# A decoder on one core: smaller four-bit scales, one product on GpSimd, and another start for the slots

## The reference

```python
def fp4_quant_dequant(x):                      # the part that the change touches
    xb = x.reshape(shape[:-1] + (shape[-1] // 16, 16))
    scale = jnp.max(jnp.abs(xb), axis=-1, keepdims=True) / 6.0
    scale = jnp.maximum(scale, jnp.float32(1e-12))
    xn = xb / scale
    idx = jnp.searchsorted(_MID, jnp.abs(xn))  # 0.25 0.75 1.25 1.75 2.5 3.5 5.0
    return (_GRID[idx] * jnp.sign(xn) * scale).reshape(shape)   # 0 0.5 1 1.5 2 3 4 6

gate = fp4_linear(x, w_gate)                   # both sides quantized
y = fp4_linear(x, w_up)
h = jax.nn.silu(gate) * y
return fp4_linear(h, w_down)

x = _layernorm(x + L0_attn(x)); x = _layernorm(x + L0_xattn(x, ctx)); x = _layernorm(x + L0_ffn(x))
x = _layernorm(x + L1_attn(x)); x = _layernorm(x + L1_xattn(x, ctx)); x = _layernorm(x + L1_ffn(x))
```

## Time and profile before

| what | us |
|---|---|
| median of 3 runs (lowest, highest) | 1032.47 (1031.52, 1033.19) |
| the profiled execution | 1034.37 |
| its span, from first to last instruction | 1032.5 |
| PE busy / PEld busy | 902.5 / 719.3 |
| DVE busy | 637.8 |
| ACT busy | 487.1 |
| POOL busy | 273.2 |

### The profile page before, as it was taken

How to read it: one execution, slowest core, us unless ns; L and a number is a source line. 1 busy time by engine, 2 the same in 40 slices (tenths; PEclk the granted TensorE clock), 3 DMA queues, 4 the chain that set the end, 5 groups by cost and what they waited for, 6 DMA issues and landing times.

```text
span 1032.5 us, 20172 instructions
## 1 busy us (share of the span) xinstructions
PE 902.5 (87%) x7498; PEld 719.3 (70%) x7498; DVE 637.8 (62%) x1909; ACT 487.1 (47%) x1127; POOL 273.2 (26%) x416
## 2 busy tenths in 40 slices
PE   4569889998999989999999989999999999598980
PEld 3346667776776766677688767777888888587870
DVE  4998877666575778786776668787653533015006
ACT  2335445445645554454454556555555454143430
POOL 4322311211152133221213222242221224024222
PEclk9678999999999988999999999999999999799995
DMA  9998000000010000000000030232112268797954
GB/s 330 386 330 296 1 2 6 11 11 11 17 46 22 17 17 21 17 6 11 7 11 22 16 113 22 83 129 98 58 46 83 79 202 274 308 331 276 377 194 161
DMA packets 39426, 114.88 MB, mean 111 GB/s; under 512 B 5464, under 2 KB 21600, under 8 KB 38688
## 3 DMA queue, kind: packets, MB, share of 16 engines
q1 hardware_dynamic: 35584, 103.35, 29.1%
q0 software_dynamic: 3744, 10.24, 2.7%
HBM read 99.13 MB, written 37.59 MB: 132 GB/s over the span
## 4 chain that ended last, share of the span: by engine, by line
PE 66%; DVE 14%; ACT 7%; issue 5%; DMA 4%; SPq 3%; POOL 0%; POOLq 0%; ACTq 0%; DVEq 0%
PE ps L693 44%; PE ps L698 8%; PE ps L705 6%; PE ps L769 3%; ACT PT L1417 2%; DMA EW<-moe_w 2%; PE ps L836 1%; ACT slot_rows L1417 1%; PE ps L994 1%; PE ps L879 1%; DVE slot_rows L1340 1%; DVE PT L1098 1%; SPq L1837 1%; DMA slot_rows<-ys_d 1%; SPq L1842 1%
## 5 line engine op out<-in xcount | busy, mean ns | idle before, releaser
L1588 POOL TENSOR_TENSOR stat<-stat,mhalf 128x1 f32<-128x1 f32 x112 | 67.5, 603 | 302.5 <-DVE stat L1035 302.3
L693 PE MATMUL ps<-wall,slot_rows 128*128 128x256 f32 (+1 forms) x448 | 135.9, 431 | 9.6 <-ACT KB L1444 4.8
L693 PEld LDWEIGHTS ps<-wall,slot_rows 128*128 128x128 f32 x448 | 80.4, 197 | 31.9 <-issue 16.5
L698 PE MATMUL ps<-cst,PT 128*128 128x128 f32 x512 | 75.8, 284 | 15.3 <-DVE PT L1089 6.7
L1098 DVE TENSOR_REDUCE PT<-ps 128x8 f32<-128x1024 f32 x64 | 75.4, 1220 | 19.8 <-PE ps L705 19.7
L705 PEld LDWEIGHTS ps<-KB 16*128 16x128 f32 (+1 forms) x2048 | 65.2, 189 | 30.1 <-issue 26.0
L705 PE MATMUL ps<-KB 16*128 16x128 f32 (+1 forms) x2048 | 77.2, 287 | 8.8 <-ACT slot_rows L1417 3.8
L698 PEld LDWEIGHTS ps<-cst,PT 128*128 128x128 f32 x512 | 60.3, 146 | 30.8 <-issue 21.1
L693 PE MATMUL ps<-wgu,slot_rows 128*128 128x352 f32 x256 | 78.8, 460 | 3.0 <-ACT PT L1417 1.9
L693 PE MATMUL ps<-slot_rows,wall 128*128 128x128 f32 x640 | 77.9, 277 | 2.6 <-ACT PT L1417 1.8
L693 PEld LDWEIGHTS ps<-slot_rows,wall 128*128 128x128 f32 x640 | 74.4, 192 | 6.6 <-ACT PT L1417 2.0
(11 more groups left out here) (221 smaller groups left out, 1843.9 us busy)
## 6 DMA issues: line engine op xcount, KB each, us to landing
EW<-moe_w SPq DMA_DIRECT2D x30, 514.0 KB
EW<-moe_w SPq DMA_DIRECT2D x30, 512.0 KB
PT<-moe_w SPq DMA_DIRECT2D x12, 514.0 KB
PT<-moe_w SPq DMA_DIRECT2D x12, 512.0 KB
wall<-wts SPq DMA_DIRECT2D x1, 4104.0 KB, 19.8
work<-xs_d SPq DMA_DIRECT2D x31, 128.5 KB
slot_rows<-ys_d SPq DMA_DIRECT2D x8, 384.0 KB, 7.8
KB<-ys_d SPq DMA_DIRECT2D x8, 384.0 KB, 6.3
```

Source lines behind the costliest of these rows:

```text
L693: last = k.e.matmul(o, a, b, start=(i == 0), stop=(i == len(pairs) - 1))
L698: last = k.e.transpose(ps[:, u.at, c * P:(c + 1) * P], src[:, c * P:(c + 1) * P], ident)
L1588: return k.e.tensor_tensor(v[:, 7:8], v[:, 8:9], mhalf[:, :], ALU.pow)
```

## The change

Three edits. (1) The scale is made positive and a little larger at once (SIXTH instead of 1/6), and the scaling of its reciprocal is gone; the sign is put right in the tail, by a subtraction instead of an addition. (2) The last product of the sample's input goes from VectorE to GpSimd; TensorE's transpose waits for GpSimd's count instead of VectorE's. (3) In the planner's lists a slot's first piece needs the Q of the sample in front instead of its transposed input, and the costs follow edits 1 and 2.

```diff
-BELOW = 1.0 - 2.0 ** -23
+SIXTH = float(np.float32((1.0 + 2.0 ** -23) / 6.0))
...
-VECTOR = [... "normed", "xn", "xq", "xn", "hy", ...
+VECTOR = [... "normed", "xn", "xy", "xn", "hy", ...
-GPSIMD = [... "turned", "turned", "root", "hq", "hq", ...
+GPSIMD = [... "turned", "turned", "root", "xq", "hq", "hq", ...
...
 def plan_sample(n):
-    yield piece(work=[("D", 0.72, None), ("A", 0.7, None)], needs=[(n, "x"), *[(n - 1, "xT", 0)] * (0 < n < NS)],
+    yield piece(work=[("D", 0.72, None), ("A", 0.7, None)], needs=[(n, "x"), *[(n - 1, "q", 0)] * (0 < n < NS)],
                 alone=n < NS)
...
     yield from plan_attention(n, 0, True)
-    yield piece(work=[("D", 1.6, None), ("A", 0.42, None)])
-    yield piece(work=[("D", 1.33, None)])
+    yield piece(work=[("D", 1.42, None), ("A", 0.42, None)])
+    yield piece(work=[("D", 0.9, None), ("P", 0.75, None)])
     yield piece(0.25, [(n, "xqT")], [("A", 0.37, (n, "xqT"))])
-    yield piece(2.45, gu[:1], [("A", 0.55, None), ("D", 0.42, gu[0]), ("D", 1.95, (n, "h"))], ["wgu"])
+    yield piece(2.45, gu[:1], [("A", 0.55, None), ("D", 0.42, gu[0]), ("D", 1.75, (n, "h"))], ["wgu"])
...
-    yield piece(work=[("D", 0.42, gu[1]), ("D", 1.95, None)], needs=[(n, "silu")])
+    yield piece(work=[("D", 0.42, gu[1]), ("D", 1.75, None)], needs=[(n, "silu")])
...
 def plan_weights():
     for i in range(9):
-        yield piece(work=[("D", 2.25, None), ("A", 0.63, ("abs", i))], needs=...
+        yield piece(work=[("D", 2.07, None), ("A", 0.63, ("abs", i))], needs=...
...
# pe_sample
-            k.wait_ge(vector[s], count(VECTOR, n, "xq"))
+            k.wait_ge(gpsimd[s], count(GPSIMD, n, "xq"))
             pe_transpose(k, u, Y[:, s, :])
...
# dve_fp4_head
-            k.after(k.step(e.tensor_scalar(sc, am, -1.0 / 6.0, -1e-12, ALU.mult, ALU.min)))
+            k.after(k.step(e.tensor_scalar(sc, am, SIXTH, 1e-12, ALU.mult, ALU.max)))
             k.after(k.step(e.reciprocal(ri, sc)))
-            k.after(k.step(e.tensor_scalar(ri, ri, -BELOW, None, ALU.mult)))
...
# dve_fp4_tail
-            k.after(k.step(e.scalar_tensor_tensor(out=xn, in0=y, scalar=1.5 * BIG, in1=xn, op0=ALU.max, op1=ALU.add)))
+            k.after(k.step(e.scalar_tensor_tensor(out=xn, in0=y, scalar=1.5 * BIG, in1=xn, op0=ALU.max, op1=ALU.subtract)))
...
# dve_sample
             k.wait_ge(scalar[s], count(SCALAR, n, "abs"))
-            k.after(k.step(dve_fp4_tail(k, fp4_x(s))))
-            dve_fp4_scale(k, Y[:, s, :], D, fp4_x(s), small).then_inc(vector[s], 1)
+            dve_fp4_tail(k, fp4_x(s)).then_inc(vector[s], 1)
...
# pool_sample, after the attention
             yield
+            y = v3(fp4_x(s)[1], DH)
+            k.wait_ge(vector[s], count(VECTOR, n, "xy"))
+            e.tensor_tensor(v3(Y[:, s, :], DH), y, bc(sm[:, s, 0, 1, 0:H].unsqueeze(2), H, DH), ALU.mult).then_inc(
+                gpsimd[s], 1)
             yield
```

More of the change, by code:

```diff
@@ L106, in use @@
         return Fill(at, prior, self.full[at], self.out[at], self.full[at + 1] if tiled else 0)
-VECTOR = ["scanned", "scanned", "ss", "var", "normed", "roped", "roped", "var", "normed", "xn", "xq", "xn", "hy", "xn", "hy",
+VECTOR = ["scanned", "scanned", "ss", "var", "normed", "roped", "roped", "var", "normed", "xn", "xy", "xn", "hy", "xn", "hy",
           "var", "normed", "var", "normed", "k1", "var", "normed", "var", "normed", "var", "normed"]
 SCALAR = ["squared", "squared", "v", "abs", "silu", "silu", "abs", "abs", "gelu", "v"]
-GPSIMD = ["rs", "root", "with bo", "turned", "turned", "root", "hq", "hq", "root", "root", "root", "twice", "root",
+GPSIMD = ["rs", "root", "with bo", "turned", "turned", "root", "xq", "hq", "hq", "root", "root", "root", "twice", "root",
           "with bo", "root"]
@@ L218, in plan_weights @@
     for i in range(9):
-        yield piece(work=[("D", 2.25, None), ("A", 0.63, ("abs", i))], needs=[("w4", i // 4), *[("wq", i - 2)] * (i > 1)],
+        yield piece(work=[("D", 2.07, None), ("A", 0.63, ("abs", i))], needs=[("w4", i // 4), *[("wq", i - 2)] * (i > 1)],
                     alone=True)
```

## The result

The changed kernel takes 1015.44 us in the median of 4 runs (1013.71 to 1015.80), beside 1032.83 us for the kernel before in the same session (4 runs, 1031.52 to 1034.70): a ratio of 0.9827 (95% interval 0.9808 to 0.9846), or 17.4 us less. The profiled execution took 1013.71 us with a span of 1011.9, 20.6 less than the span before.

The account below looks back on a forecast made before the run. TensorE was taken as the main bound, VectorE as the bound from 22 to 79 us. The terms -2.1 - 1.7 + 0.73 = -3.07 us led from 1032.47 to 1029.4 us, range 1021.5 to 1036.5 (the forecast's own 1027.6 to 1031.5).

Parts of the forecast that it names:

- the sum's -2.1 and -1.7: L1052's removed 0.21 us steps on the chain: ten in the front, -2.1 us; eight behind 110 us, -1.7 us.
- The lower bound given behind 110 us: Eight L1052 steps behind 110 us gain nothing instead of 1.7 us if TensorE has other samples' work there.
- counted at nothing: Sixteen L1062 products leave VectorE, 5.6 us off the chain, hidden by TensorE's work from 130 to 870 us: no gain.
- +0.73 us for the scan that leaves a hole: Scan pair at 15.83 us moves from VectorE's idle hole behind the first Q, into the VectorE-bound front: +0.73 us.
- what this sum leaves open: All five queues may come out in another order from the first slot on; called larger than the sum, not counted.
- the sign given for a wrong forecast: TensorE's idle time from the full stage's start to the last routing moving by more than 3 us from about 40.
- gaps close: Rival: new order cuts TensorE's idle time at 300 to 450 us from 14.6 to 6.8, another -7.8 us, 1021.6 us; chance 0.22.
- gaps open: Rival: samples fall in step at 130 to 300 us, idle at 9.7% instead of 5.8%, +6.7 us, 1036.1 us; chance 0.26.
- What the front gains before 870 us reaches the end whole.: Everything behind 870 us hangs on the last sample's routing, and no removed or moved work lies behind it.
- The tail unchanged within 1 us: The stretch behind the second batch's table, expert tiles and joins, was to keep its length within 1 us.
- Contention: Rival: GpSimd's 16 new products stretch VectorE's instructions, 5.8 us, 1.8 on the path, 1031.2 us; chance 0.12.
- the fourth rival: Planner may start the slots where they were, so the 0.73 us fall away: 1028.7 us; no chance of its own.

Follow-up runs that it names:

- third: Kernel before with six planner list costs moved by 0.02 to 0.06 us, no instruction changed: 1016.39 us, ratio 0.984.
- the five kernels of the table: Before; changed; changed's lists with the work of before; before with six list costs moved; changed with product's list cost 0.62: spans 1032.5, 1011.9, 1023.9, 1015.4, 1032.6 us.

## Why the prediction was wrong

| order | work of before | edit 1 | edits 1 and 2 |
|---|---|---|---|
| old | 1032.1 to 1033.0 | 1028.80 | 1029.30 |
| new | 1029.03 | 1020.70 | 1015.44 (the change) |
| third | 1016.39 | 1014.38 | 1013.74 |

**Edit 1, the sum's -2.1 and -1.7: right in size under the order that it was read from.** 4.2 us measured where 3.8 stood. The split was off: the front gave all of it (3.6 us at slot 5's start with edit 1 alone, 103.93 to 100.34; 3.1 with both edits), and the eight steps on the chain behind 110 us, counted at 1.7, added 0.5 us with both edits (3.1 to 3.6 us of lead at the table) and 1.3 with edit 1 alone (3.6 to 4.9). On VectorE's queue 13 L1052 steps stand ahead of slot 5's scan, 2.7 us, where the chain had nine of them; the rest of the 3.6 is not explained. The lower bound given behind 110 us, that TensorE has other samples' work at those places, is nearer to what was seen. Two errors of opposite sign cancelled, and the agreement of 4.2 with 3.8 is in part luck. One reservation: with both edits TensorE's idle time over the whole span is 129.7 us, as before (130.0), and the span is shorter by busy time, so from one profiled execution of each it can't be said through which of the two the lead reached the end.

**Edit 2, counted at nothing: right under the old order as far as the runs can tell, wrong in the new one**, where it brought 5.3 us (0.7 to 9.9). The cost side: the new product of the changed kernel (ns lowest/median/highest, first and last start us),

```profile
L1640 POOL TENSOR_TENSOR Y<-PT,sm x16: 610/621/837, 76.6 to 690.8; 128x256 f32<-128x256 f32 x16
```

is 0.62 us in the median where 0.74 was taken from GpSimd's addition of that size. TensorE waited for the new product once, 1.5 us. What the work queued behind it on GpSimd cost was not measured by itself.

**Edit 3, +0.73 us for the scan that leaves a hole: not measured.** The scan pair moved behind the Q addition, as forecast; in the changed kernel's VectorE timeline:

```profile
20.40 0.42 DVE L1252 TENSOR_TENSOR row<-row,ps 128x256 f32<-128x256 f32 x1 [4.49 <-PE ps L693]
21.07 0.68 DVE L1049 TENSOR_REDUCE X<-EW 128x32 f32<-128x512 f32 x1
...
23.17 0.42 DVE L1077 TENSOR_TENSOR slot_rows<-ps,row 128x256 f32<-128x256 f32 x1
23.84 0.73 DVE L1128 TENSOR_TENSOR_SCAN slot_rows<-lam,Y 128x128 f32<-128x128 f32 x2
```

The addition that ends the hole starts at 20.40 us instead of 21.84, but that is no work of the edits. The same ten products stand ahead of it on TensorE in both traces, and the last four took longer in the kernel before (line L693 from 15 to 24 us: ns lowest/median/highest, first and last start; before, then after), though the profile gives a granted clock of 1.00 from 16 to 22 us in both:

```profile
L693 PE MATMUL ps<-wall,X x4: 591/634/634, 19.9 to 21.2; 128*128 128x256 f32 x4
L693 PE MATMUL ps<-wall,X x4: 378/380/380, 19.3 to 20.0; 128*128 128x256 f32 x4
```

It differs by chance from one execution to the next: over the 16 traces this addition starts between 20.40 and 21.88 us. Under the old order it starts at 20.65 with edits 1 and 2 and at 21.87 with edit 1 alone, two kernels with the same work up to there, and it starts at 21.88 in the changed kernel with the operation put back. That scatter is twice the term, so whether the 0.73 us was paid can't be read. It also shifts what lies behind it by up to as much: of the 4.1 us at slot 5's start between the two kernels of the new order, 0.35 were there at this addition (20.75 and 20.40). The last weight part's head, whose end the prediction had "about 2 us earlier less 0.73", reaches its product at 70.48 us against 74.83, 4.35 us earlier. With the work of before the new order has it at 73.74, so 1.1 us came with the order and 3.3 with the removed work.

**The order: the step that failed.** It was in the text as "what this sum leaves open" and entered the sum at nothing; it was bounded by letting one stretch idle at the rate of its neighbour: -7.8 us for 300 to 450 us, as a rival of chance 0.22. The runs showed 3.7 us for the order alone and, with it, 13.6 us for the removed work instead of 3.5. Three things were wrong with the bound. It was one stretch's, and TensorE's idle time from 130 us to the last table fell by 13.9 us, nearly all of it in the three others (the sign given for a wrong forecast was more than 3). The argument against was that TensorE's longest wait was for ScalarE, "which the change does not relieve"; an order relieves it without giving the engine less to do, and the waits for the exponential fell by half, 19.8 to 9.4 us, nearly all of it (to 10.0) with the order alone. And the order's gain was added to a fixed value of the removed work. Order alone, 3.7 us, and work alone, 3.5, make 7.2 of the 17.4 measured; the other 10 are there only with both. An order fixes which instructions lie on the path, so the value of every removed instruction is a property of the order too.

One more thing was overlooked, by the prediction and after it. "No row shows the new order" is true of the trace, but the planner is in the kernel's source, and its own clock can be read before any run. This is the time at which orders_of places the end of the last output, for each of the nine orders, beside the measured median (where several versions share an order, the one whose instructions the lists describe):

| order | planner's end, us | measured, us |
|---|---|---|
| changed, "dn" cost other | 998.9 | 1013.86 |
| changed, three costs other | 999.8 | 1023.04 |
| new (the change) | 1003.1 | 1015.44 |
| third | 1004.6 | 1016.39 |
| changed, product's cost 0.62 | 1011.6 | 1031.55 |
| old (before) | 1012.1 | 1032.1 to 1033.0 |
| edit 3 alone | 1013.9 | 1039.10 |
| edits 1 and 3 | 1018.9 | 1036.92 |
| edits 1 and 2 | 1023.4 | 1036.38 |

The four orders that it ends below 1005 us measured 1014 to 1023 us, and the five above 1011 measured 1032 to 1039; the six that were not picked by it for these runs (all but the first two and the third order) fall the same way. Within a group it does not sort. For the change it gave -9.0 us, a reason to hold "gaps close" for likelier than "gaps open", where the prediction had 0.22 and 0.26.

**"What the front gains before 870 us reaches the end whole."** Wrong as soon as the order moves: the stretch behind the table took 163.1, 170.7, 169.3, 167.5 and 177.2 us in the five kernels of the table, where 720, 768, 767, 748 and 800 products were left for it. Nor does the table decide: with "dn" at 0.94 it comes at 870.43 us, later than before, and only 143.1 us follow. "The tail unchanged within 1 us" missed 7.6.

**The rivals.** Gaps close: the right direction and mechanism, its size and place too small. Gaps open: not this change, but three of the draws around it (edit 3 alone, edits 1 and 2, edits 1 and 3) end slower than before, at 1036.4 to 1039.1 us, where the price given was 1036.1. The condition (TensorE idle over 45 us) was not met in the changed kernel. Contention: little, and not as priced. VectorE's L1050 in the sample blocks went from 8.9 us (186 ns in the mean) in the kernel before to 10.5 for 48 in the changed one:

```profile
L1050 DVE TENSOR_SCALAR sm<-sm 128x22 f32<-128x22 f32 (+1 forms) x48 | 10.5, 219 | 1.6
```

But with the product on GpSimd under the old order it is still 186 ns, and in the new order without that product 204. So about half of the rise comes with the new order alone, and the product adds to it only there. Under the old order the product added 0.5 us to the time (1029.30 against 1028.80), and the runs leave that some 2.6 us either way, so the price of 1.8 us is not seen and not excluded. The change does what it says, so the fourth rival fell.

**What stays open.** Which placements in the order close the gaps was not found; the experiments show that a list number moved by 0.02 to 0.13 us carries the end by up to 16 us, not which pair of pieces does it. Open too are what the choice of banks has in it and why TensorE's granted clock differs between the orders. Three versions have lower medians than the changed kernel (1013.74, 1013.86 and 1014.38 us), all within its interval; none is shown to beat it. They do beat the kernel before, and six moved list costs without any edited instruction come within 1 us of the change.

## What to carry to other kernels

Where a planner writes the queues from costs, every edit of a cost or a need writes the whole order anew. Here the times spread from 1014 to 1039 us, while the removed work was worth 3 to 4 us under the old order. Read the planner's own end time for the new lists before forecasting: it told fast orders from slow ones, though not the best from the second. Test the instructions under a frozen order and the order under frozen instructions before crediting either, and keep the lists frozen (or search them on purpose) when work is taken out. An idle gap that waits for an engine which the change leaves alone is no argument that the gap will stay.

## What the hardware showed beyond the forecast

GpSimd's product of 128x256 with a broadcast scale took 0.62 us, against 0.42 us for VectorE's, though GpSimd's addition of the same size takes 0.745. And a VectorE instruction with two inputs in SBUF is held up beside GpSimd, which no row of before had shown. GpSimd's and VectorE's timelines of the changed kernel:

```profile
96.86 0.90 POOL L1652 TENSOR_TENSOR KB<-PT,sm 128x352 f32<-128x352 f32 x1 [1.65 <-DVE PT L1057]
```

```profile
96.70 0.42 DVE L1088 TENSOR_TENSOR PT<-PT,Y 128x256 f32<-128x256 f32 x1
97.03 1.01 DVE L1084 TENSOR_TENSOR PT<-slot_rows,cst 128x256 f32<-128x256 f32 x1
```

L1084 has the shape of L1088 ahead of it and takes 1.01 us instead of 0.42, and it ends shortly after GpSimd's product does (98.04 and 97.76). The Trainium skill, page "SBUF — State Buffer", section "Who interferes with whom", says that such instructions are blocked; this row agrees. The price that this rule gave in the prediction, 11.8 us in all and 3.7 on the path, is not there. Under the old order VectorE's busy time fell by 5.0 us (627.4 to 622.4) when 7.4 us of product left it, so some 2.4 us came back, and the time rose by 0.5 us in the medians.
